# A token shift mixed ahead of the projections on GpSimd and VectorE, and the post units one step earlier

## The chip, the cores and the metric

One core of a Trainium2 chip runs the whole program. The metric is the device time of that core in microseconds (us), as a median of several executions. A second kind of record is one profiled execution, whose trace gives the start and length of every instruction. The engines are TensorE (PE in the rows, with its weight loads as PEld), VectorE (DVE), ScalarE (ACT), GpSimd (POOL) and SyncE (SP), which only issues transfers here. Each works through its own list in order and waits on semaphores.

## What is computed

Two blocks in a row, on x of 8 batches, 512 tokens, 128 channels, each followed by a residual sum and a layer norm. The first is a causal attention of 16 heads of 8 channels, whose score is a tanh of q times k plus two bias terms. The second is a feed-forward part with a token shift, and it is the one that changes:

```python
x_prev = jnp.concatenate([jnp.zeros((B, 1, C), x.dtype), x[:, :-1, :]], axis=1)
xr = mu_r * x + (1.0 - mu_r) * x_prev
xk = mu_k * x + (1.0 - mu_k) * x_prev
r = jax.nn.sigmoid(jnp.einsum('btc,dc->btd', xr, W_r))
k = jnp.einsum('btc,dc->btd', xk, W_k)
k_act = jnp.square(jax.nn.relu(k))
out = r * jnp.einsum('btc,dc->btd', k_act, W_v)
```

mu_r and mu_k are one number per channel.

## The kernel before, in words

The work of a batch is one *period* of 20 *steps* (PAIRS). Step t belongs to pair t of the batch: two score tiles of 128 keys by up to 512 queries, packed so that causal blocks that are empty are left out. A pair goes this way:

- *scores* on TensorE: q times k into one of three PSUM places (PSUM_PAIRS) of 1024 columns. It waits until *main* has read the pair that was in that place, three pairs before.
- *tanh* on ScalarE (L784), from PSUM to the tile probs.
- *biases* on TensorE, one step later (BIAS_LAG), into the same PSUM place. It waits for the tanh.
- *main* on VectorE (L1005): alpha times tanh plus biases.
- *exp* on ScalarE (L789), three steps after its tanh (EXP_LAG), so that tanh of pair t is followed by exp of pair t-3.
- *mask* on GpSimd (L893), in the same step as exp: zeros above the diagonal. It is one or two affine_select.
- *weighted sums* on TensorE (values_of), at the steps of VALUES_STEPS, into the tile sums.

On TensorE the scores of pair t+1 come last in step t, but at the steps of AHEAD_FIRST (2, 3, 4, 7, 9, 18) they come right behind the biases.

Beside the pairs, each period carries *side units*, all through one PSUM bank (side_bank), which the reader of a unit has to free before the next. The unit tables say at which step TensorE makes them:

- PREP_UNITS and VALUES_UNITS, for a later batch: xT2, q2, k2, F2 (features), G2 (lattice features), v1. What comes of q, k, J and G is cut into three bf16 parts: *hi* (VectorE, L1039), *rest* (GpSimd, L900: subtract), *mid* (VectorE, L1044), *lo* (GpSimd, L906: subtract). SyncE writes them to DRAM and loads them from there in another layout. The tables PREP in the GpSimd and VectorE programs give the steps.
- POST_UNITS, for the batch before: oT0 and oT1 (transposes of the sums, then *normalise*), aT (transpose of the attention output), y (output projection), x1T, kk, rr, kv. Their readers are in the tables POST: on VectorE *attn_out*, *residual* with *stats* and *moments*, *x1_out* (copy of x1T from PSUM, L1105), *gate* (L1111); on GpSimd *inv_std* (L914, L916: the reciprocal root), *norm* (L924, L928), *gated_residual* (L934).

So the path from y to the output of a batch runs y, residual, stats, moments, inv_std, norm, x1T, x1_out, kk and rr, relu and square and r_tanh on ScalarE, kv, gate, gated_residual, second stats, inv_std and norm.

The tile x1T has 1+512 columns, of which the first is zero, so x1T[:, 0:512] is the input shifted by one token. The setup scales each of the two weights twice, by mu and by 1-mu (w_r_mix, w_k_mix), and kk and rr are each a sum of two products, one with x1T and one with its shifted view. All are in fp32, and each product of 512 columns stands in the trace as two matmul records. kk gives 512 tokens in one go; rr is made in four blocks of 128 tokens.

Which periods have what: period 0 has preparation and no post units. Periods 1 to 5 have all (periods 1 to 4 run in a hardware loop of two periods a turn). Period 6 and 7 have post units and no preparation, period 7 no values either. The feed-forward part of the last batch stands behind the periods, in two halves of 256 tokens, with code and semaphores of its own (tail).

In the setup VectorE's instructions are linked: each waits for the one before (link). The copies and scalings of the weights stand in front of x_out(1), which feeds the second batch's q, k and features.

## Time and profile before

| what | us |
|---|---|
| median of 3 runs | 443.48 |
| lowest and highest | 440.82, 444.28 |
| the profiled execution, whole | 439.53 |
| its span, first to last instruction | 437.5 |

The page of the profile gives the busy time of each engine, with its share of the span and its instructions:

```profile
PE 368.5 (84%) x2907; PEld 190.6 (44%) x2907; DVE 328.5 (75%) x539; ACT 327.2 (75%) x364; POOL 230.4 (53%) x367
```

and the span in 40 slices, each digit the busy share in tenths (9 is 90% or more):

```profile
PE   3657778808989999999999998999898999899863
DVE  4874778806797979788887889788977876697643
ACT  1012489915899888989898988898889998999712
POOL 4315337611388636963597349644965264435541
PEclk9855899957999999999999999999999999899978
```

The first quarter is setup and period 0, with a gap at about 90 to 100 us in which TensorE waits for a transfer. From about 100 to 412 us run the seven periods with post units, then the tail. TensorE's granted clock is full through the periods.

### The profile page before, as it was taken

The page shows a single profiled execution, that of the slowest core. Times are in us where ns is not written, and L with a number is a line of the kernel's source. Part 1 is how long each engine was busy: PE and PEld are TensorE (multiplying, and loading weights), DVE is VectorE, ACT ScalarE, POOL GpSimd, SP SyncE. Part 2 cuts the span into 40 slices and gives each one's busy share as a digit, 9 for nine tenths or more (in the row PEclk, how much of TensorE's full clock was granted, in tenths as well). Part 3 has the DMA queues.
Part 4 walks back from the last instruction along what each step waited for, and adds up shares of the span by engine and source line. Part 5 has one row for each costly group of instructions (what it writes and reads, how often), then busy time and mean ns, then how long its engine had stood idle before and what let it go on. Part 6 is the DMA issues. An engine that isn't in the chain of part 4 may idle for free.

```text
span 437.5 us, 8760 instructions
## 1 busy us (share of the span) xinstructions
PE 368.5 (84%) x2907; PEld 190.6 (44%) x2907; DVE 328.5 (75%) x539; ACT 327.2 (75%) x364; POOL 230.4 (53%) x367
## 2 busy tenths in 40 slices
PE   3657778808989999999999998999898999899863
PEld 1232333304446444544445354645353546344543
DVE  4874778806797979788887889788977876697643
ACT  1012489915899888989898988898889998999712
POOL 4315337611388636963597349644965264435541
PEclk9855899957999999999999999999999999899978
DMA  3357878678766376758763876676755751100000
GB/s 97 112 167 152 200 192 137 123 171 183 123 146 198 101 149 125 150 147 181 141 159 111 172 143 136 169 167 142 146 149 139 151 111 40 49 25 1 2 25 24
DMA packets 40272, 55.31 MB, mean 126 GB/s; under 512 B 3427, under 2 KB 38243, under 8 KB 38655
## 3 DMA queue, kind: packets, MB, share of 16 engines
q1 hardware_dynamic: 36542, 53.06, 52.9%
q10 hardware_dynamic: 3696, 1.84, 2.4%
q8 instruction: 18, 0.29, 0.3%
q14 instruction: 16, 0.12, 0.1%
HBM read 38.69 MB, written 16.19 MB: 125 GB/s over the span
## 4 chain that ended last, share of the span: by engine, by line
PE 42%; DVE 18%; issue 9%; POOL 9%; DMA 9%; SPq 6%; ACT 5%; ACTq 0%; DVEq 0%; POOLq 0%
PE raw L512 16%; PE side_bank L512 14%; PE sums L512 9%; DVE probs L1005 7%; DMA i_stack<-hamming_i 5%; SPq L413 3%; DMA k_rows<-parts 3%; ACT probs L789 3%; ACT probs L784 2%; POOL probs L893 2%; PE side_bank L599 2%; POOL x L928 2%; POOL x L924 2%; POOL parts L906 2%; DVE bn L1090 1%
## 5 line engine op out<-in xcount | busy, mean ns | idle before, releaser
L1005 DVE SCALAR_TENSOR_TENSOR probs<-probs,scal,raw 128x1024 f32<-128x1024 f32 x160 | 202.2, 1272 | 46.2 <-PE raw L512 45.7
L784 ACT ACTIVATE probs<-raw 128x1024 f32<-128x1024 f32 x160 | 163.9, 1025 | 52.0 <-PE raw L512 51.3
L893 POOL TENSOR_SCALAR_AFFINE_SELECT probs<-probs 128x256 f32<-128x256 f32 (+1 forms) x224 | 98.8, 459 | 150.7 <-ACT probs L789 150.2
L789 ACT ACTIVATE probs<-probs 128x1024 f32<-128x1024 f32 x160 | 169.3, 1059 | 0.9 <-DVE probs L1005 0.9
L512 PE MATMUL raw<-q_stack,k_stack 72*128 72x384 bf16 (+3 forms) x512 | 99.0, 306 | 17.3 <-DVE probs L1005 13.7
L512 PE MATMUL raw<-i_stack,j_stack 111*128 111x384 bf16 (+3 forms) x512 | 98.0, 304 | 15.1 <-DMA i_stack<-hamming_i 12.5
L512 PE MATMUL sums<-probs,values 128*32 128x256 f32 (+2 forms) x1280 | 93.0, 390 | 4.2 <-POOL probs L893 4.1
L512 PEld LDWEIGHTS raw<-q_stack,k_stack 72*128 72x128 bf16 x512 | 38.5, 99 | 71.3 <-DVE probs L1005 46.4
L512 PEld LDWEIGHTS raw<-i_stack,j_stack 111*128 111x128 bf16 x512 | 42.3, 98 | 60.2 <-issue 31.9
L512 PEld LDWEIGHTS sums<-probs,values 128*32 128x32 f32 x1280 | 29.5, 108 | 50.4 <-issue 26.0
L900 POOL TENSOR_TENSOR whole<-whole,parts 128x512 f32<-128x512 f32 x22 | 26.1, 1188 | 22.8 <-DVE parts L1039 22.8
L906 POOL TENSOR_TENSOR parts<-whole,parts 128x512 bf16<-128x512 f32 x30 | 35.1, 1172 | 4.2 <-DVE parts L1044 4.2
L1068 DVE COPY sums_sb<-sums 128x512 f32<-128x512 f32 x15 | 10.4, 691 | 19.9 <-PE sums L512 19.9
L1044 DVE CAST parts<-whole 128x512 bf16<-128x512 f32 x32 | 16.7, 522 | 2.9 <-POOL whole L900 2.8
L916 POOL TENSOR_TENSOR rstd<-var_eps,minus_half 128x4 f32<-128x4 f32 x14 | 14.7, 1047 | 1.2
L512 PEld LDWEIGHTS side_bank<-w_r_mix,x1T 128*128 128x128 f32 x112 | 13.6, 191 | 1.0
L797 ACT ACTIVATE feats<-side_bank 128x512 f32<-128x512 f32 x8 | 4.9, 612 | 12.1 <-PE side_bank L512 12.1
L512 PE MATMUL side_bank<-w_r_mix,x1T 128*128 128x128 f32 x112 | 13.6, 275 | 0.0
L1039 DVE CAST parts<-whole 128x512 bf16<-128x512 f32 x24 | 12.2, 508 | 1.9 <-DMA q_rows<-parts 1.6
L512 PE MATMUL side_bank<-x1T,w_k_mix 128*128 128x512 f32 x28 | 13.2, 591 | 0.0
L836 ACT ACTIVATE probs<-shift_col 1x1536 bf16<-1x1536 bf16 x1 | 1.5, 1481 | 14.9 <-DVE w_r_mix L1245 14.9
L1090 DVE BATCH_NORM_STATS2 bn<-res 128x6 f32<-128x128 f32 x56 | 12.2, 279 | 0.2
(144 smaller groups left out, 345.7 us busy)
## 6 DMA issues: line engine op xcount, KB each, us to landing
q_stack<-q_rows SPq DMA_DIRECT2D x21, 384.0 KB
k_stack<-k_rows SPq DMA_DIRECT2D x21, 384.0 KB
i_stack<-lattice_i SPq DMA_DIRECT2D x21, 288.0 KB
i_stack<-hamming_i SPq DMA_DIRECT2D x21, 288.0 KB
q_rows<-parts SPq DMA_DIRECT2D x8, 384.0 KB, 17.2
k_rows<-parts SPq DMA_DIRECT2D x8, 384.0 KB, 8.9
j_rows<-parts SPq DMA_DIRECT2D x8, 384.0 KB, 8.5
lattice_i<-parts SPq DMA_DIRECT2D x8, 288.0 KB
```

The source lines that it names most:

```text
L413: sp.dma_start(i_stack[par][at:at + rows, first:first + n], lattice_i[par].rearrange("l (e h) i -> (l e) (h i)", h=H)[:, first:first + n]) ...
L512: return nc.tensor.matmul(o, lhsT, rhs, start=start, stop=stop, **kw)
L784: nc.scalar.activation(pair_probs(t), raw[:, t % PSUM_PAIRS, :].rearrange("p (u i) -> p u i", u=2), ACT.Tanh).then_inc(tanh_done, 1)
L789: nc.scalar.activation(pair_probs(t), pair_probs(t), ACT.Exp).then_inc(exp_done, 1)
L893: last = nc.gpsimd.affine_select(out=v, in_=v, compare_op=ALU.is_ge, fill=0.0, base=0, pattern=[[0, v.shape[1]], [1, P]], channel_multipli ...
L900: nc.gpsimd.tensor_tensor(whole[:, kind, :], feats[:] if kind == J else whole[:, kind, :], parts[:, kind, 0, :], ALU.subtract).then_inc(re ...
L906: nc.gpsimd.tensor_tensor(parts[:, kind, 2, :], whole[:, kind, :], parts[:, kind, 1, :], ALU.subtract).then_inc(lo_done[kind], 1)
L916: nc.gpsimd.tensor_tensor(rstd[:], var_eps[:], minus_half[:], ALU.pow).then_inc(rstd_done, 1)
L1005: v.scalar_tensor_tensor(out=o, in0=o, scalar=scal[:, 2:3], in1=raw[:, t % PSUM_PAIRS, :].rearrange("p (u i) -> p u i", u=2), op0=ALU.mult ...
L1039: v.tensor_copy(parts[:, kind, 0, :], feats[:] if kind == J else whole[:, kind, :]).then_inc(hi_done[kind], 1)
L1044: v.tensor_copy(parts[:, kind, 1, :], whole[:, kind, :]).then_inc(mid_done[kind], 1)
L1090: v.bn_stats(bn[:, blk, :], res[:, blk, :]).then_inc(bn_done, 1)
```

## The change

kk and rr become single products, of the unscaled weights (w_kT, w_rT) with inputs that are mixed beforehand: mix = x_prev + mu times (x - x_prev). The difference x - x_prev is one subtraction on GpSimd (*shifted*, tile shift_dif), the two mixes are scalar_tensor_tensor on VectorE (*mix*, for k first). They are written into tiles that are free at that time, attnT and the second half of sums_sb. kk and rr wait for the mixes (mix_done) where they waited for x1_out. The setup gets two more copies, of the unscaled weights; the scaled ones stay, for the tail, which is unchanged.

The post units from aT on move one step forward, v1 one back, G2 one forward. The tables of VectorE and GpSimd are set anew, for the preparation too. The core of the diff:

```diff
-PREP_UNITS = {0: ["xT2"], 2: ["q2"], 3: ["k2"], 5: ["F2"], 12: ["G2"]}
+PREP_UNITS = {0: ["xT2"], 2: ["q2"], 3: ["k2"], 5: ["F2"], 11: ["G2"]}
...
-VALUES_UNITS = {7: ["v1"]}
+VALUES_UNITS = {8: ["v1"]}
-POST_UNITS = {1: ["oT0"], 6: ["oT1"], 8: ["aT"], 10: ["y"], 14: ["x1T"], 16: ["kk"], 17: ["rr"], 18: ["kv"]}
+POST_UNITS = {1: ["oT0"], 6: ["oT1"], 7: ["aT"], 9: ["y"], 13: ["x1T"], 15: ["kk"], 16: ["rr"], 17: ["kv"]}
...
+        shift_dif = sb("shift_dif", [P, T])
+        mixed = [attnT[:], sums_sb[:, 1, :]]
...
-                    pe.wait_ge(dve_freed, side_units.through(b, "x1T"))
-                    mm(o, w_k_mix[0][:], x1T[:, 1:1 + T], stop=False)
-                    last = mm(o, w_k_mix[1][:], x1T[:, 0:T], start=False)
+                    pe.wait_ge(mix_done[1], pv + 1)
+                    last = mm(o, w_kT[:], mixed[1])
                 elif use == "rr":
-                    pe.wait_ge(dve_freed, side_units.through(b, "x1T"))
-                    for n in range(JB):
-                        mm(o[:, n * P:(n + 1) * P], x1T[:, 1 + n * P:1 + (n + 1) * P], w_r_mix[0][:], stop=False)
-                        last = mm(o[:, n * P:(n + 1) * P], x1T[:, n * P:(n + 1) * P], w_r_mix[1][:], start=False)
+                    pe.wait_ge(mix_done[0], pv + 1)
+                    last = four(o, mixed[0], w_rT[:])
...
+            def shifted(n):
+
+                pool.wait_ge(dve_freed, side_units.through(n + 1, "x1T"))
+                nc.gpsimd.tensor_tensor(shift_dif[:], x1T[:, 1:1 + T], x1T[:, 0:T],
+                                        ALU.subtract).then_inc(dif_done, 1)
...
-            PREP = {6: [(rest, Q)], 10: [(lo, Q), (rest, K)], 13: [(lo, K), (rest, J)], 14: [(rest, G)],
-                    16: [(lo, J)], 17: [(lo, G)]}
...
+            PREP = {6: [(rest, Q)], 8: [(lo, Q)], 11: [(rest, K)], 12: [(rest, J)], 14: [(rest, G)], 15: [(lo, K)],
+                    16: [(lo, J)], 18: [(lo, G)]}
...
+            def mix(n):
+
+                dve.wait_ge(dif_done, n + 1)
+                for which in (1, 0):
+                    v.scalar_tensor_tensor(out=mixed[which], in0=shift_dif[:], scalar=mu[:, which:which + 1],
+                                           in1=x1T[:, 0:T], op0=ALU.mult, op1=ALU.add).then_inc(mix_done[which], 1)
...
+            PREP = {0: [(x_out,)], 2: [(projected, Q)], 3: [(projected, K)], 5: [(hi, Q)], 7: [(mid, Q)], 10: [(hi, K)],
+                    11: [(features_i,), (hi, J)], 12: [(mid, K), (hi, G)], 15: [(mid, J)], 16: [(mid, G)]}
...
+                link(v.tensor_copy((w_rT, w_kT)[n][:], src))
```

How the lists stand on the engines, at three places of a full period. The first is GpSimd, behind the first half of the normalisation of x1: the rest of it, the masks, and the bf16 cutting of J, K and G. Before:

```order
L928 TENSOR_TENSOR x<-x,rstd 128x512 [waits centred,rstd_done]
L890 REGISTER_ALU
L893 AFFINE_SELECT probs<-probs 128x4x128 [waits exp_done]
L890 REGISTER_ALU
L893 AFFINE_SELECT probs<-probs 128x2x128 [waits exp_done]
L906 TENSOR_TENSOR parts<-whole,parts 128x512 [waits mid_done1]
L900 TENSOR_TENSOR whole<-feats,parts 128x512 [waits hi_done2]
```

and after:

```order
L930 TENSOR_TENSOR x<-x,rstd 128x512 [waits centred,rstd_done]
L892 REGISTER_ALU
L895 AFFINE_SELECT probs<-probs 128x2x128 [waits exp_done]
L895 AFFINE_SELECT probs<-probs 128x2x128
L902 TENSOR_TENSOR whole<-whole,parts 128x512 [waits hi_done1]
L892 REGISTER_ALU
L895 AFFINE_SELECT probs<-probs 128x4x128 [waits exp_done]
L902 TENSOR_TENSOR whole<-feats,parts 128x512 [waits hi_done2]
L892 REGISTER_ALU
L895 AFFINE_SELECT probs<-probs 128x2x128 [waits exp_done]
L935 ISA
L936 TENSOR_TENSOR shift_dif<-x1T 128x512 [waits dve_freed]
```

The normalisation is now followed by mask 8 (the two pieces), rest K (L902 with hi_done1), mask 9, rest J and mask 10, and then the new subtraction (L936). Before, rest K stood ahead of the root, and mask 8 between the root and the normalisation, where mask 7 stands now.

The second is VectorE from step 12 on, between the mains (probs). Before:

```order
L1005 SCALAR_TENSOR_TENSOR probs<-probs,scal,raw 128x1024 [waits tanh_done,bias_ready]
L1039 CAST parts<-whole 128x512 [waits scratch_in3,dve_freed]
L1002 REGISTER_ALU
L1005 SCALAR_TENSOR_TENSOR probs<-probs,scal,raw 128x1024 [waits tanh_done,bias_ready]
L1016 REGISTER_ALU
L1105 COPY x1T<-side_bank 128x512 [waits dve_unit]
L1068 COPY sums_sb<-sums 128x512 [waits pv_done]
L1002 REGISTER_ALU
L1005 SCALAR_TENSOR_TENSOR probs<-probs,scal,raw 128x1024 [waits tanh_done,bias_ready]
```

and after:

```order
L1053 CAST parts<-whole 128x512 [waits rest_done1]
L1048 CAST parts<-whole 128x512 [waits scratch_in3,dve_freed]
L1011 REGISTER_ALU
L1014 SCALAR_TENSOR_TENSOR probs<-probs,scal,raw 128x1024 [waits tanh_done,bias_ready]
L1025 REGISTER_ALU
L1114 COPY x1T<-side_bank 128x512 [waits dve_unit]
L1011 REGISTER_ALU
L1014 SCALAR_TENSOR_TENSOR probs<-probs,scal,raw 128x1024 [waits tanh_done,bias_ready]
L1120 SCALAR_TENSOR_TENSOR sums_sb<-shift_dif,mu,x1T 128x512 [waits dif_done]
L1120 SCALAR_TENSOR_TENSOR attnT<-shift_dif,mu,x1T 128x512
```

mid K (L1053, waits rest_done1) is new in this place, and the two mixes (L1120) stand behind the main of pair 13, in front of the copy of the sums and the main of pair 14. They wait for the subtraction.

The third is TensorE around kk. Before:

```order
L512 MATMUL raw<-q_stack,k_stack 128x512 [waits scores_done]
L512 MATMUL raw<-q_stack,k_stack 128x512
L550 REGISTER_ALU
L512 MATMUL raw<-i_stack,j_stack 128x512 [waits tanh_done]
L512 MATMUL raw<-i_stack,j_stack 128x512
L610 REGISTER_ALU
L512 MATMUL side_bank<-x1T,w_k_mix 128x512 [waits dve_freed]
L512 MATMUL side_bank<-x1T,w_k_mix 128x512
L568 REGISTER_ALU [waits mask_done]
L512 MATMUL sums<-probs,values 32x256 [waits sums_read]
L512 MATMUL sums<-probs,values 32x256 x3
```

and after:

```order
L517 MATMUL raw<-i_stack,j_stack 128x256 [waits tanh_done]
L517 MATMUL raw<-i_stack,j_stack 128x256 x3
L615 REGISTER_ALU
L517 MATMUL side_bank<-sums_sb,w_kT 128x512 [waits mix_k_done,dve_freed]
L517 MATMUL sums<-probs,values 32x256 [waits mask_done]
L517 MATMUL sums<-probs,values 32x256 x3
L517 MATMUL raw<-q_stack,k_stack 128x512 [waits scores_done]
L517 MATMUL raw<-q_stack,k_stack 128x512
L555 REGISTER_ALU
L517 MATMUL raw<-i_stack,j_stack 128x512 [waits tanh_done]
L517 MATMUL raw<-i_stack,j_stack 128x512
```

kk is one product, waits for the mix of k, and stands ahead of the scores of pair 16 (the 128x512 q_stack row behind it); before, those scores stood ahead of kk.

## Rows read from the trace of the kernel before

**Rows 1.** Table of stretches: stretch, length, busy us (count) per engine, PEclk, DMA.

```profile
241.00:286.00 45.00, 42.66 (x361) 22.42 (x360) 38.15 (x61) 39.84 (x44) 28.85 (x45) 1.00 0.69 151
```

**Rows 2.** Groups by line and form: engine, names, shapes, count, busy us, mean ns, idle.

```profile
L512 PE MATMUL side_bank<-w_r_mix,x1T 128*128 128x128 f32 x112 | 13.6, 275 | 0.0
...
L512 PE MATMUL side_bank<-x1T,w_k_mix 128*128 128x512 f32 x28 | 13.2, 591 | 0.0
...
L900 POOL TENSOR_TENSOR whole<-whole,parts 128x512 f32<-128x512 f32 x22 | 26.1, 1188 | 22.8 <-DVE parts L1039 22.8
...
L1111 DVE SCALAR_TENSOR_TENSOR gated<-r_tanh,side_bank 128x512 f32<-128x512 f32 x7 | 4.8, 687 | 0.7
```

**Rows 3.** Timeline, ScalarE: start, length, instruction, and in brackets the idle time before.

```profile
235.47 1.03 ACT L784 ACTIVATE probs<-raw 128x1024 f32<-128x1024 f32 x1 [1.06 <-PE raw L512]
...
255.40 1.02 ACT L784 ACTIVATE probs<-raw 128x1024 f32<-128x1024 f32 x1 [1.53 <-PE raw L512]
...
272.11 0.60 ACT L799 ACTIVATE k_act<-side_bank 128x512 f32<-128x512 f32 x1
...
273.28 1.01 ACT L784 ACTIVATE probs<-raw 128x1024 f32<-128x1024 f32 x1
...
275.92 1.02 ACT L784 ACTIVATE probs<-raw 128x1024 f32<-128x1024 f32 x1
...
277.77 1.03 ACT L784 ACTIVATE probs<-raw 128x1024 f32<-128x1024 f32 x1
...
280.72 1.02 ACT L784 ACTIVATE probs<-raw 128x1024 f32<-128x1024 f32 x1 [0.98 <-PE raw L512]
```

**Rows 4.** Timeline, TensorE: scores of pair 9, x1T, kk.

```profile
254.76 0.60 PE L512 MATMUL raw<-q_stack,k_stack 72*128 72x256 bf16 x4
...
266.84 0.63 PE L599 MATMUL side_bank<-ident,x 128*128 128x128 f32 x4 [0.46 <-POOL x L928]
...
270.17 1.88 PE L512 MATMUL side_bank<-x1T,w_k_mix 128*128 128x512 f32 x4
```

**Rows 5.** Timeline, VectorE: main of pair 9, residual, moments, mid K, x1_out.

```profile
258.39 1.26 DVE L1005 SCALAR_TENSOR_TENSOR probs<-probs,scal,raw 128x1024 f32<-128x1024 f32 x1
259.58 0.68 DVE L1102 TENSOR_TENSOR res<-side_bank,x_res 128x512 f32<-128x512 f32 x1
...
261.32 0.38 DVE L1097 BATCH_NORM_AGGREGATE mean_var<-bn 128x2 f32<-128x6 f32 x4 [0.15 <-DVE bn L1090]
...
262.79 0.42 DVE L1044 CAST parts<-whole 128x512 bf16<-128x512 f32 x1
...
268.08 0.68 DVE L1105 COPY x1T<-side_bank 128x512 f32<-128x512 f32 x1
```

**Rows 6.** Timeline, GpSimd: inv_std, norm of x1, masks 9 and 10.

```profile
262.37 0.25 POOL L914 TENSOR_SCALAR var_eps<-mean_var 128x4 f32<-128x4 f32 x1
...
264.45 1.05 POOL L924 TENSOR_TENSOR x<-res,mean_var 128x512 f32<-128x512 f32 x1
...
266.64 1.19 POOL L893 TENSOR_SCALAR_AFFINE_SELECT probs<-probs 128x512 f32<-128x512 f32 x2
```

**Rows 7.** Timelines of VectorE, TensorE and ScalarE in period 6.

```profile
347.74 0.68 DVE L1102 TENSOR_TENSOR res<-side_bank,x_res 128x512 f32<-128x512 f32 x1
...
357.85 1.88 PE L512 MATMUL side_bank<-x1T,w_k_mix 128*128 128x512 f32 x4
...
368.47 1.02 ACT L784 ACTIVATE probs<-raw 128x1024 f32<-128x1024 f32 x1 [1.06 <-PE raw L512]
```

**Rows 8.** The chain that ended last: start, length, what; then TensorE's timeline.

```profile
31.15 0.30 DVE w_vT L1247
...
78.27 21.64 DMA i_stack<-hamming_i
...
100.04 1.03 PE L512 MATMUL raw<-i_stack,j_stack 111*128 111x512 bf16 x2 [12.53 <-DMA i_stack<-hamming_i]
```

**Rows 9.** Timelines of GpSimd and VectorE in the setup: the subtraction beside a cast.

```profile
22.85 1.53 POOL L906 TENSOR_TENSOR parts<-whole,parts 128x512 bf16<-128x512 f32 x1 [2.79 <-DVE parts L1044]
...
23.40 1.26 DVE L1044 CAST parts<-whole 128x512 bf16<-128x512 f32 x1
```

16 lines of the change are left out of this document (9 added, 7 removed).

## The prediction

> **What bounds the kernel now.** I read the table of stretches first, then the timeline of each engine over one of the five full periods of the loop. In the 45 us from 241 to 286, TensorE is busy 42.66, ScalarE 39.84, VectorE 38.15, GpSimd 28.85 [rows 1]. A matmul's end is modelled, so 95% for TensorE doesn't say that its work is the limit. ScalarE has 39.84 of work and so about 5.2 us of waiting, and every one of its longer waits is for scores from TensorE. It gives the period its pace: tanh and exp of a pair take 1.85 us, start to start (275.92 to 277.77) [rows 3]. A period is 45.25 us, from tanh of pair 0 at 235.47 to the next at 280.72 [rows 3].
>
> Where do ScalarE's waits stand? 1.06 us before pair 0, 1.53 before pair 9 (255.40), 0.98 before the next pair 0 (280.72), the rest in small pieces [rows 3]. Around the two projections that the change halves, ScalarE hardly waits: from the relu at 272.11 on to the tanh at 277.77 it works through, and 0.98 is what it waits at the end [rows 3]. So two engines are full there at once, and what TensorE saves is worth only what ScalarE waits.
>
> The second thing to see is the chain that feeds the feed-forward part, on three in-order engines: y on TensorE, residual and statistics on VectorE (259.58 to 261.70), reciprocal root and normalisation on GpSimd (262.37 to 266.64), the transpose x1T on TensorE, which sat 0.46 us for it (266.84), then kk at 270.17 [rows 4, 5, 6]. This chain already ends a wait on TensorE.
>
> **The change, part by part.** I use three points of a period: R, where VectorE starts the residual (259.58), K, where kk starts (270.17), T, the next tanh of pair 0 (280.72). Before: R to K 10.6, K to T 10.55 [rows 3, 4, 5].
>
> TensorE loses half of kk and of rr: 13.2 and 13.6 us in 7 periods, so 1.89 and 1.94 each, and half of both is 1.9 us a period [rows 2]. GpSimd gains one 128x512 subtraction of two SBUF tiles: the like one (L900) takes 1.19 on average [rows 2]. VectorE gains two 128x512 scalar_tensor_tensor that read SBUF alone. No row shows this exact form in the loop; the nearest is the gate, 0.69 with one PSUM input [rows 2]. I take 0.69, 1.38 for both. ScalarE's work is unchanged.
>
> *R moves.* y goes to step 9, where its TensorE place is in front of what used to be step 10. The scores of pair 9, on which ScalarE waited the 1.53, keep their place: between them and step 6 stand the same products, only in another order (aT before, v1 after the two groups of weighted sums). They start at 254.76 [rows 4]. Scores 9 and biases 8 at no more than 0.6 each end at 255.96, main of pair 8 on VectorE takes 1.19 (258.39 to 259.58), so R comes at about 257.1, 2.5 earlier [rows 4, 5]. The casts moved on VectorE (mid and hi of Q and K) are in other gaps of it and cost nothing there.
>
> *R to K grows.* Statistics 2.12 (259.58 to 261.70) [rows 5]. GpSimd, now free, goes on at once: 2.08 for the root and the mask behind it (262.37 to 264.45; mask 8 there, mask 7 after, both of two pieces), 2.19 for the normalisation (to 266.64) [rows 6]. Up to here R+6.4. But what stood ahead of the normalisation on GpSimd now stands behind it: mask 8 (a mask of two pieces is about 0.7 of those 2.08), rest K 1.19, masks 9 and 10 1.19 (the two of 266.64), rest J 1.19, and only then the new subtraction, 1.19 [rows 2, 6]. By GpSimd alone: 6.4+0.7+4x1.19 = R+11.9, and with the first mix (0.69) kk starts at R+12.6. By VectorE it is a little later: its mid K, at step 12, waits for rest K at R+8.3, while VectorE would be there at R+6.9 (2.12, three mains at 1.19, and 1.2 for two casts and a copy between them). It stands 1.4 us with main of pair 12 queued behind. Then two casts 0.7 (0.42 each, their ends overlapped), main 12 1.19, the x1T copy 0.68, the subtraction 1.2, the mix 0.7 [rows 2, 5]: R+12.85. I take 12.85, so K is at 270.0 where it was at 270.17, though its place in the program is one pair earlier. That is the core of my forecast: the chain and not TensorE sets when kk starts, and the step forward is paid back as an idle TensorE ahead of kk, with the scores of pair 16 queued behind it and ScalarE waiting for those, and for kk's relu, about 1.2 us.
>
> *K to T.* kk alone 0.95, relu and square 1.17 (272.11 to 273.28), then ScalarE works through four pairs and r_tanh. From 273.28 to 277.77 it did two pairs and r_tanh with 0.19 of waiting, 4.49, so four pairs and r_tanh are 4.3+3.7 = 8.0 [rows 3]. Together 10.2 against 10.55: the halved rr and the 0.98 wait give 0.35, and no more. A further 0.1 to 0.2 may come at pair 1.
>
> A full period: -2.5+2.25-0.35 = -0.6 us, 44.65. Five of them: -3.0.
>
> *The last two periods* have no preparation, so no rest K and no rest J on GpSimd. R there is 347.74, kk 357.85, T 368.47 with 1.06 of waiting [rows 7]. R moves 1.7 earlier (pair 9 waited less there). R to K: R+6.4 for the normalisation, transpose and copy to R+7.7, masks to R+8.3, subtraction to R+9.5; but main of pair 13 holds VectorE until R+10.2 because its biases came late behind the waiting transpose, so kk at R+10.9, against 10.1. ScalarE is then still busy with the pairs before, and T comes 0.9 earlier, pair 1 about 1.7. I take 1.3: -2.6 for two.
>
> *Setup.* Two more 128x128 copies out of PSUM stand in the linked chain before x_out(1); the like one takes 0.30 and 0.02 to 0.04 between them. That chain runs on into the DMA that TensorE waits for until 100.04, 78.27 to 99.91 [rows 8]. So +0.7 at most, 0 if a full DMA queue swallows it. I take 0.7. The last batch's feed-forward part, behind the loop, is as before.
>
> Sum: -3.0-2.6+0.7 = -4.9 us on the profiled execution of 439.5, which gives 434.6. That execution is 4 us under the median of the runs shown, 443.48; on the median the same difference gives 438.6.
>
> **A rule against the change.** In the setup a GpSimd tensor_tensor took 1.53 (its like in the loop 1.19) and a cast on VectorE beside it took 1.26, where it takes 0.42 otherwise [rows 2, 5, 9]. So a VectorE operation can be held for up to 0.84 us beside GpSimd. Both mixes run while GpSimd goes on to mask 11 and rest G. If the first is held so, kk is 0.84 later. The Trainium skill, "GPSIMD Engine Reference", section "Key points", says that GpSimd shares its SBUF interfaces with VectorE and contends with instructions of two SBUF inputs, which the mixes are and the gate (0.69) is not; by it the mixes cost more than the row I used. The trace bears the contention out for casts; the one two-input form can't be separated there.
>
> **The rivals.**
> A, *TensorE was the limit.* For it: 42.66 of 45 busy. Against it: ScalarE doesn't wait around kk and rr. If GpSimd's chain is shorter than my sum, or VectorE has slack where I have none, the whole 1.9 us a period comes out, 7 times: -13.3+0.7, 430.9. Chance 0.2.
> B, *the mixes are held by GpSimd*: +0.84 on R to K in seven periods, +5.9 on my forecast, 444.5, no change. Chance 0.12.
> C, slower: *VectorE and GpSimd wait for each other.* In a full period K may be at most R+13.45 before the period gets longer than it was. If the subtraction slips behind one more exp (mask 10 ahead of it waits for exp 10, the mix holds the mains, they hold the exps), one pair's time, 1.85, is lost in each full period: -0.6+1.85 = +1.25, five times +6.2, and with nothing gained in the last two +6.9 in all: 450.4. Against it: exp 10 is over about 2 us before its mask's turn by my order of things. Chance 0.18.
> My forecast, 0.5.
>
> **How the numbers follow.** About 1% (4.4 us) is what a measurement can tell here. My -4.9 stands just beyond it, so the forecast's half divides 0.3 faster, 0.2 same. Faster: 0.3+0.2 = 0.5. Same: 0.2+0.12 = 0.32. Slower: 0.18. The forecast's own range is 435.5 to 442; with A at 430.9 and B at 444.5 inside and half of C cut off, 430 to 446.
>
> **What would show it.** In the changed profile: TensorE idle 1 to 1.7 us ahead of kk with the mix as releaser, ScalarE's wait moved from pair 0 to the relu or pair 16; VectorE idle about 1.4 us before mid K for rest K; R at pair 9's main, GpSimd without a gap from the root to the subtraction; kk one record pair instead of two, rr 8 records; the mixes 0.69. Period near 44.65, kk to kk. If TensorE doesn't wait for the mix and the period is near 43.4, A holds. If the mixes take over 0.9, B. If kk comes later than R+13.45, C. My forecast is wrong if R is not 2 us earlier relative to T.

## The result, and the profile after

The changed kernel takes 467.19 us (median of 4 runs, 463.74 to 471.20) where the kernel before takes 442.15 (4 runs, 435.68 to 444.28): a ratio of 1.063, with a 95% interval of 1.041 to 1.085. Some executions of a kernel fall in a slower state of the chip (the profiled ones of the changed kernel, of mixing alone, of mid K at 13 and of rr at 14 on VectorE did); every ratio here compares the other executions alone, and so isn't the quotient of the two medians beside it. Forecast were 438.6 us and a range of 430 to 446. The profiled execution took 471.2 us, its span 469.5 against 437.5, so the traces have 32.0 us to explain. This execution is the slowest of the four. The medians are 25 us apart and the ratio stands for 27.8 us, so 4 to 7 of the 32.0 are scatter between executions.

The page of the changed kernel: busy time by engine, and the row of TensorE's granted clock in 40 slices.

```profile
PE 375.0 (80%) x2837; PEld 185.9 (40%) x2837; DVE 348.5 (74%) x555; ACT 329.0 (70%) x364; POOL 241.5 (51%) x374
...
PEclk9856899858979999789979998899978999999997
```

TensorE has 70 records fewer and yet is busy 6.5 us longer (375.0 against 368.5). That can't be work; the last row says what it is: a 7 or 8 in nine of the slices 10 to 39, where the row of before has three. The table of stretches over one full period (columns as in [rows 1]: stretch, length, busy us and count of TensorE, its weight loads, VectorE, ScalarE and GpSimd, the clock, the DMA) puts it in its place:

```profile
254.70:277.00 22.30, 21.43 (x177) 11.26 (x175) 18.68 (x24) 19.97 (x22) 10.23 (x19) 1.00 0.65 142
...
286.30:291.20 4.90, 1.48 (x6) 0.64 (x6) 4.90 (x6) 3.11 (x4) 3.29 (x5) 0.77 0.61 114
291.20:296.00 4.80, 4.76 (x16) 1.60 (x17) 3.09 (x3) 1.93 (x3) 3.21 (x4) 0.52 0.57 125
296.00:304.00 8.00, 7.22 (x79) 4.34 (x77) 6.92 (x16) 7.45 (x9) 5.55 (x8) 1.00 0.33 118
```

From 286.3 to 291.2 TensorE works 1.48 us of 4.90, while VectorE is busy all the time. In the 4.8 us after it TensorE is busy throughout at a clock of 0.52, which is nearly all at the lower of its levels, 1.2 GHz. ScalarE has 3.11 and 1.93 us of work in these two stretches together of 9.7; in all of [rows 1] it waited some 5 us in 45. The timelines of the same period, engine by engine. ScalarE, to be held against [rows 3]:

```profile
254.75 1.03 ACT L786 ACTIVATE probs<-raw 128x1024 f32<-128x1024 f32 x1 [1.72 <-PE raw L517]
...
289.19 1.02 ACT L786 ACTIVATE probs<-raw 128x1024 f32<-128x1024 f32 x1 [1.75 <-PE raw L517]
...
293.32 0.60 ACT L801 ACTIVATE k_act<-side_bank 128x512 f32<-128x512 f32 x1 [2.17 <-PE side_bank L517]
...
295.30 1.02 ACT L786 ACTIVATE probs<-raw 128x1024 f32<-128x1024 f32 x1 [0.72 <-PE raw L517]
...
305.41 1.03 ACT L786 ACTIVATE probs<-raw 128x1024 f32<-128x1024 f32 x1 [1.65 <-PE raw L517]
```

TensorE, to be held against [rows 4]:

```profile
283.40 0.63 PE L604 MATMUL side_bank<-ident,x 128*128 128x128 f32 x4 [0.78 <-POOL x L930]
...
288.53 0.62 PE L517 MATMUL raw<-q_stack,k_stack 72*128 72x512 bf16 x2 [2.30 <-DVE probs L1014]
...
291.24 2.04 PE L517 MATMUL side_bank<-sums_sb,w_kT 128*128 128x512 f32 x2 [1.24 <-DVE sums_sb L1120]
...
304.77 0.61 PE L517 MATMUL raw<-q_stack,k_stack 72*128 72x512 bf16 x2 [1.55 <-DVE probs L1014]
```

VectorE, to be held against [rows 5] (residual, mid K, hi G, main of pair 12, x1T, the two mixes, second statistics, main of pair 18):

```profile
276.60 0.69 DVE L1111 TENSOR_TENSOR res<-side_bank,x_res 128x512 f32<-128x512 f32 x1 [0.16 <-PE side_bank L517]
...
285.15 0.83 DVE L1053 CAST parts<-whole 128x512 bf16<-128x512 f32 x1 [1.60 <-POOL whole L902]
285.91 1.37 DVE L1048 CAST parts<-whole 128x512 bf16<-128x512 f32 x1
287.20 1.27 DVE L1014 SCALAR_TENSOR_TENSOR probs<-probs,scal,raw 128x1024 f32<-128x1024 f32 x1
288.39 0.68 DVE L1114 COPY x1T<-side_bank 128x512 f32<-128x512 f32 x1
...
290.23 0.87 DVE L1120 SCALAR_TENSOR_TENSOR sums_sb<-shift_dif,mu,x1T 128x512 f32<-128x512 f32 x1
291.02 1.64 DVE L1120 SCALAR_TENSOR_TENSOR attnT<-shift_dif,mu,x1T 128x512 f32<-128x512 f32 x1
...
302.12 0.88 DVE L1099 BATCH_NORM_STATS2 bn<-res 128x6 f32<-128x128 f32 x4 [0.55 <-POOL res L942]
...
303.45 1.26 DVE L1014 SCALAR_TENSOR_TENSOR probs<-probs,scal,raw 128x1024 f32<-128x1024 f32 x1
```

GpSimd, to be held against [rows 6] (rest K, mask, rest J, then the new subtraction, mask, rest G):

```profile
283.96 1.16 POOL L902 TENSOR_TENSOR whole<-whole,parts 128x512 f32<-128x512 f32 x1
285.08 0.63 POOL L895 TENSOR_SCALAR_AFFINE_SELECT probs<-probs 128x512 f32<-128x512 f32 x1
285.68 1.32 POOL L902 TENSOR_TENSOR whole<-feats,parts 128x512 f32<-128x512 f32 x1
...
289.16 1.04 POOL L936 TENSOR_TENSOR shift_dif<-x1T 128x512 f32<-128x512 f32 x1 [1.61 <-DVE x1T L1114]
290.14 0.41 POOL L895 TENSOR_SCALAR_AFFINE_SELECT probs<-probs 128x256 f32<-128x256 f32 x1
290.52 1.59 POOL L902 TENSOR_TENSOR whole<-whole,parts 128x512 f32<-128x512 f32 x1
```

There are two stalls. **The first**: VectorE stands 1.60 us for rest K (until 285.15), and from the start of its first cast to the start of the main of pair 12 behind them pass another 2.05 us. TensorE has its scores of pair 15 waiting for that main, and stands 2.30 us. Then kk waits 1.24 more for the subtraction and the mix, and runs at half clock: two records take 2.04 us, about as long as the four of before at full clock (1.88, [rows 4]). What the change saved on kk is not there. **The second**: at 302.12 the second statistics stand on VectorE ahead of the main of pair 18. The next period's scores of pair 0 take the place in raw that this main frees; TensorE stands 1.55 us ahead of 304.77.

The last two periods, against [rows 7], in the timelines of VectorE, TensorE and ScalarE:

```profile
377.15 0.69 DVE L1111 TENSOR_TENSOR res<-side_bank,x_res 128x512 f32<-128x512 f32 x1
...
388.52 1.10 PE L517 MATMUL side_bank<-sums_sb,w_kT 128*128 128x512 f32 x2 [0.80 <-DVE sums_sb L1120]
...
400.59 1.02 ACT L786 ACTIVATE probs<-raw 128x1024 f32<-128x1024 f32 x1 [1.70 <-PE raw L517]
```

The first stall isn't there (no rest K, no rest J) and kk is really halved, 1.10 us. The second is there in full, 1.70 before pair 0. In the setup, against [rows 8], TensorE is released by the transfer at 99.42, where it was at 100.04:

```profile
99.42 1.03 PE L517 MATMUL raw<-i_stack,j_stack 111*128 111x512 bf16 x2 [11.58 <-DMA i_stack<-hamming_i]
```

With kk as a mark (starts in the timelines at 137.19, 188.15, 240.97, 291.24, 341.87, 388.52, 433.18; before at 133.65, 178.98, 224.84, 270.17, 315.59, 357.85, 400.61) the 32.0 us divide so: 3.5 up to the first kk, 22.7 over four full periods (51.17 against 45.49 each), 6.3 over the two that end with the last kk, and -0.6 behind it. The 3.5 are -0.6 up to the release above and +4.2 from there to the first kk, which aren't taken apart here. The release alone scatters from 92.7 to 102.2 over the traces of all the kernels below.

### The profile page after: what moved, and what is told of

Same layout as the page of the kernel before. It is cut to its first block, busy times and chain, and to the rows that moved or that the text cites. A ratio compares the mean times of both kernels' runs of the same rounds, so it can differ in the third digit from the quotient of the medians.

```text
span 469.5 us, 8647 instructions
## 1 busy us (share of the span) xinstructions
PE 375.0 (80%) x2837; PEld 185.9 (40%) x2837; DVE 348.5 (74%) x555; ACT 329.0 (70%) x364; POOL 241.5 (51%) x374
## 4 chain that ended last, share of the span: by engine, by line
PE 38%; DVE 22%; issue 10%; DMA 8%; POOL 8%; ACT 7%; SPq 5%; DVEq 0%; POOLq 0%; ACTq 0%
PE raw L517 15%; PE side_bank L517 12%; PE sums L517 9%; DVE probs L1014 8%; ACT probs L791 5%; DMA i_stack<-hamming_i 4%; SPq L418 3%; DMA k_rows<-parts 3%; DVE parts L1048 2%; POOL probs L895 2%; PE side_bank L604 2%; POOL res L942 2%; DVE bn L1099 2%; ACT probs L786 2%; POOL whole L902 1%
## 5 line engine op out<-in xcount | busy, mean ns | idle before, releaser
L895 POOL TENSOR_SCALAR_AFFINE_SELECT probs<-probs 128x256 f32<-128x256 f32 (+1 forms) x224 | 100.5, 462 | 160.4 <-ACT probs L791 160.3
L517 PE MATMUL raw<-q_stack,k_stack 72*128 72x384 bf16 (+3 forms) x512 | 103.0, 315 | 32.8 <-DVE probs L1014 30.6
L517 PE MATMUL raw<-i_stack,j_stack 111*128 111x384 bf16 (+3 forms) x512 | 102.2, 313 | 14.3 <-DMA i_stack<-hamming_i 11.6
L517 PE MATMUL sums<-probs,values 128*32 128x256 f32 (+2 forms) x1280 | 96.5, 402 | 1.5 <-POOL probs L895 1.3
L902 POOL TENSOR_TENSOR whole<-whole,parts 128x512 f32<-128x512 f32 x22 | 28.3, 1285 | 24.0 <-DVE parts L1048 24.0
L1053 DVE CAST parts<-whole 128x512 bf16<-128x512 f32 x32 | 18.3, 573 | 10.0 <-POOL whole L902 9.9
L517 PE MATMUL side_bank<-sums_sb,w_kT 128*128 128x512 f32 x14 | 12.4, 984 | 8.7 <-DVE sums_sb L1120 8.7
L1048 DVE CAST parts<-whole 128x512 bf16<-128x512 f32 x24 | 15.1, 628 | 0.9 <-DMA q_rows<-parts 0.7
L604 PE MATMUL side_bank<-ident,x 128*128 128x128 f32 x56 | 8.8, 279 | 6.9 <-POOL x L930 5.4
L517 PE MATMUL side_bank<-xT,wqT 128*128 128x512 f32 x14 | 10.6, 848 | 3.4 <-DVE xT L1029 2.9
```

Source lines behind the costliest of these rows:

```text
L517: return nc.tensor.matmul(o, lhsT, rhs, start=start, stop=stop, **kw)
L604: last = nc.tensor.transpose(o[:, n * P:(n + 1) * P], src(n), ident[:])
L895: last = nc.gpsimd.affine_select(out=v, in_=v, compare_op=ALU.is_ge, fill=0.0, base=0, pattern=[[0, v.shape[1]], [1, P]], channel_multipli ...
L902: nc.gpsimd.tensor_tensor(whole[:, kind, :], feats[:] if kind == J else whole[:, kind, :], parts[:, kind, 0, :], ALU.subtract).then_inc(re ...
L1048: v.tensor_copy(parts[:, kind, 0, :], feats[:] if kind == J else whole[:, kind, :]).then_inc(hi_done[kind], 1)
L1053: v.tensor_copy(parts[:, kind, 1, :], whole[:, kind, :]).then_inc(mid_done[kind], 1)
```

## The experiments

Fifteen kernels, in four groups; each group ran on one chip, beside the kernel before, and its ratios are against those runs. Beside each ratio with its 95% interval stand the starts of the first and the fifth kk in the trace, the mean period between them (their difference by 4), and the longest repeated waits of TensorE within a full period, in us. A wait named kk or rr stands ahead of that product; a number alone is a wait for a main where it is over 1, and for a mask or the normalised x1 where it is under. The four ratios of the first group (statistics at 19, mid K at 13, steps alone, mixing alone) rest on only three executions of the kernel before. The periods are those of one trace each.

| kernel | us | ratio [interval] | 1st, 5th kk | period | TensorE's wait |
|---|---|---|---|---|---|
| before | 437.07 to 442.15 | 1 | 133.65, 315.59 | 45.49 | 0.56 |
| after | 467.19 | 1.063 [1.041, 1.085] | 137.19, 341.87 | 51.17 | 2.30, 1.55, kk 0.8 to 1.7 |
| statistics at 19 | 453.90 | 1.043 [1.034, 1.053] | 129.99, 327.71 | 49.43 | 2.30, kk 0.8 to 1.7 |
| mid K at 13 | 456.53 | 1.044 [1.030, 1.058] | 135.00, 331.72 | 49.18 | kk 2.21, 1.54 |
| both moves | 443.47 | 1.018 [1.006, 1.030] | 131.33, 316.74 | 46.35 | kk 2.21 |
| both, rest G later | 442.05 | 1.013 [1.002, 1.023] | 131.43, 318.22 | 46.70 | kk 2.21 |
| steps alone | 464.69 | 1.070 [1.056, 1.084] | 132.00, 333.36 | 50.34 | 2.30, 1.54 |
| steps alone, repaired | 434.99 | 0.993 [0.990, 0.997] | 131.08, 310.47 | 44.85 | 0.79 |
| mixing alone | 460.62 | 1.047 [1.033, 1.062] | 139.91, 336.52 | 49.15 | kk 3.46 |
| zeros, too many | 459.30 | 1.051 [1.038, 1.064] | 135.05, 333.30 | 49.56 | 1.49 |
| zeros, sized | 454.69 | 1.037 [1.030, 1.045] | 133.16, 327.56 | 48.60 | 1.49, kk 0.81 |
| rr alone mixed | 434.60 | 0.993 [0.988, 0.998] | 127.74, 308.07 | 45.08 | 0.54, rr 0.25 |
| same, on VectorE | 433.37 | 0.991 [0.988, 0.995] | 134.94, 316.15 | 45.30 | 0.54 |
| repaired, rr at 15 | 457.29 | 1.047 [1.042, 1.052] | 128.29, 320.33 | 48.01 | rr 2.31 |
| repaired, rr at 14 | 438.51 | 0.998 [0.994, 1.002] | 131.71, 313.06 | 45.34 | 1.01 |
| same, on VectorE | 437.14 | 0.994 [0.990, 0.998] | 134.91, 316.25 | 45.34 | 1.01 |
| both mixed, on VectorE | 451.62 | 1.031 [1.027, 1.036] | 136.12, 329.00 | 48.22 | kk 3.05 |

### Which part of the change loses: steps alone, mixing alone

Steps alone: the tables of the changed kernel, the products of before, no subtraction and no mixes.

```diff
-                    pe.wait_ge(mix_done[1], pv + 1)
-                    last = mm(o, w_kT[:], mixed[1])
+                    pe.wait_ge(dve_freed, side_units.through(b, "x1T"))
+                    mm(o, w_k_mix[0][:], x1T[:, 1:1 + T], stop=False)
+                    last = mm(o, w_k_mix[1][:], x1T[:, 0:T], start=False)
...
```

> The changed kernel's tables with the products as before (two for kk, sixteen records for rr), no subtraction and no mixes. Theory P (the tables' places are most of the loss: statistics ahead of main 18, mid K waiting for rest K): the mixes' chain of about 2.7 us ahead of kk is gone, but 1.9 us of products are back and both waits stay; about 455 to 460. Theory M (the mixing is the loss): about 442, as before, or less.

464.69 us, ratio 1.070: theory P in kind, though it had expected 455 to 460. The loss is there whole with nothing of the mixing. VectorE's wait (1.60) and casts (0.83, 1.37) are the same, and so is TensorE's wait of 2.30 ahead of the scores of pair 15. In the timeline of TensorE and in the table of stretches of this kernel, one of the periods in which the four products of kk took twice their time:

```profile
281.19 1.04 PE L517 MATMUL raw<-q_stack,k_stack 72*128 72x512 bf16 x2 [2.29 <-DVE probs L1017]
...
282.87 3.62 PE L517 MATMUL side_bank<-x1T,w_k_mix 128*128 128x512 f32 x4
```

```profile
281.00:287.00 6.00, 5.81 (x18) 2.16 (x18) 1.92 (x3) 2.44 (x3) 2.69 (x4) 0.50 0.52 103
```

In two of the five full periods kk takes 3.62, in the others 1.88, and the wait ahead of the scores of pair 15 is 2.29 to 2.30 in all five.

Mixing alone: the tables of before, the products of the changed kernel; the subtraction is last at step 14 of GpSimd, behind rest G, the mixes at step 15 of VectorE.

```diff
-            POST = {10: [(inv_std, 0)], 11: [(norm, 0)], 18: [(gated_residual,)], 19: [(inv_std, 1), (norm, 1)]}
+            POST = {10: [(inv_std, 0)], 11: [(norm, 0)], 14: [(shifted,)], 18: [(gated_residual,)],
+                    19: [(inv_std, 1), (norm, 1)]}
...
```

> The new projections (subtraction on GpSimd at step 14, mixes on VectorE at 15, single products) in the tables of before. Theory P: kk is held by mask 11, rest G, subtraction and mix, about 1 to 2 us a period late, rr and kk are 1.9 us shorter; 442 to 450. Theory M (the mixing is the loss): 460 or more. Theory A (TensorE was the limit and only the tables spoil it): 430 to 435.

460.62 us, ratio 1.047: by its number this is theory M, by its place theory P, for it is kk that is held, and longer than the 1 to 2 us expected. So either part loses by itself, and the two don't add: TensorE stands 3.46 us ahead of kk in each full period, VectorE 0.93 for the subtraction.

### Undoing one place at a time

The second statistics back behind the main of pair 18 (step 19 of VectorE), the rest as changed:

```diff
-                    17: [(gate,)], 18: [(stats, 1, 0), (stats, 1, 1), (moments, 1)]}
+                    17: [(gate,)], 19: [(stats, 1, 0), (stats, 1, 1), (moments, 1)]}
```

> The changed kernel, with VectorE's second statistics back at step 19, behind main of pair 18. Theory P (a place in VectorE's list): the scores of the next period's pair 0 wait for main of pair 18, which the changed kernel puts behind the statistics; TensorE stood 1.54 us there. With the statistics behind it again this wait goes, about 1.5 us a period in seven periods: 10 us less than the changed kernel's 467, about 457. Theory Q (the late kk is the whole loss, what comes behind it is late in any case): within 3 us of 467.

453.90 us, ratio 1.043. The wait ahead of pair 0 is gone in every full period, the first stall stays (2.30, kk 2.05): theory P, with 13 us by the medians and 9 by the ratios for its 10. The period falls by 1.74.

Mid K one step later on VectorE, behind the main of pair 12, hi G where it is:

```diff
-                    11: [(features_i,), (hi, J)], 12: [(mid, K), (hi, G)], 15: [(mid, J)], 16: [(mid, G)]}
+                    11: [(features_i,), (hi, J)], 12: [(hi, G)], 13: [(mid, K)], 15: [(mid, J)], 16: [(mid, G)]}
```

> The changed kernel, with mid K on VectorE one step later (13), so that hi G and main of pair 12 no longer wait for rest K. Theory P: VectorE's 1.60 us wait in each of the five full periods goes, kk comes 1 to 1.5 us earlier, TensorE's 2.3 us gap ahead of the scores of pair 15 shrinks below 1 and the granted clock stays full around kk, which gives about another 1 us: 2 to 2.5 us a period, 455 to 458. Theory G (GpSimd's list, not the wait of VectorE, sets when kk starts): 464 or more.

456.53 us, ratio 1.044. The 2.30 ahead of the scores of pair 15 is gone, but the time appears ahead of kk, 2.21 us, and kk still takes 2.05 in three of five periods (1.29 and 1.34 in the others). Theory P had the time right and two of its steps wrong: it expected an earlier kk and a full clock around it. The period falls by 1.99.

Both, the two diffs above together:

> The changed kernel with both repairs: second statistics at step 19 and mid K at step 13. Theory P (the two places cost independently): 13 us from the one and 11 from the other off 467, so about 443, level with the kernel before. Theory S (the two share one loss, since each kernel's period is ended by the same chain): 450 or more.

443.47 us, ratio 1.018, as theory P had it. The period falls by 4.82, more than 1.74 and 1.99 together. (The ratios fall by 2.0, 1.9 and 4.6 points, and their intervals of one to two points each don't part 4.6 from the sum; the 1.1 us a period more is read from one trace of each.) Part of the reason is in the stretches behind the wait ahead of kk, which is 2.21 to 2.22 us in both kernels. First mid K alone moved (wait up to 282.0), then both (wait up to 271.3):

```profile
279.80:282.00 2.20, 0.02 (x1) 0.00 (x0) 1.57 (x3) 2.11 (x3) 2.20 (x4) 0.83 0.58 100
282.00:287.00 5.00, 4.97 (x16) 1.77 (x17) 3.29 (x4) 2.14 (x3) 3.20 (x4) 0.50 0.65 108
```

```profile
269.00:271.30 2.30, 0.09 (x2) 0.04 (x1) 1.67 (x3) 2.18 (x3) 2.30 (x4) 1.00 0.86 200
271.30:277.00 5.70, 5.70 (x44) 3.27 (x45) 5.38 (x7) 4.54 (x7) 4.45 (x7) 1.00 0.69 150
```

After the same wait the clock is 0.50 in the one and 1.00 in the other; kk takes 2.05 against 1.10 (1.10 to 1.49 in the five periods), and ScalarE waits 2.21 and 0.71 ahead of the relu and of pair 16 against 1.25 and nothing. These two periods are the extremes. In the 5 us from the start of kk on, the clock is 0.50, 0.66, 0.67, 0.50 and 0.66 in the five full periods with mid K alone moved, and 1.00, 0.66, 0.66, 1.00 and 0.66 with both.

The kernel with both moves prices the clock by itself. Its kk starts at 131.33, 176.79, 224.31, 271.30 and 316.74. The two periods that begin with kk at full clock last 45.46 and 45.44 us, the two that begin with 0.66 last 47.52 and 46.99, all behind the same wait of 2.21. So the fallen clock costs 1.5 to 2.1 us each time here, and where it stays up the period is no longer than before (45.49), in spite of the wait. The next kernel below agrees: one period of 45.44 that begins at full clock, and 46.85 to 47.53 for the three that begin at 0.66 to 0.69.

Rest G of GpSimd one step later than in that, behind the mixes:

```diff
-            PREP = {6: [(rest, Q)], 8: [(lo, Q)], 11: [(rest, K)], 12: [(rest, J)], 14: [(rest, G)], 15: [(lo, K)],
+            PREP = {6: [(rest, Q)], 8: [(lo, Q)], 11: [(rest, K)], 12: [(rest, J)], 15: [(rest, G), (lo, K)],
```

> Both repairs, and GpSimd's rest G moved from step 14 to 15, so that no two-input GpSimd operation stands beside the mixes. Theory Po (the second mix is held by rest G): the mix of r falls from 1.64 to 0.87 us or less, 0 to 0.8 us a period less than with both repairs alone. Theory W (a mix is 1.64 by itself): it stays.

442.05 us, ratio 1.013. The second mix falls from 1.64 to 0.74 us, so GpSimd's rest G had held it. The first stays at 0.87 and kk waits 2.21 as before; the intervals don't part the two kernels, and in the traces the period is 0.35 longer, with the clock at 1.00 behind kk in one period of five where it was in two. What holds the second mix costs nothing that can be measured, since rr comes a pair later.

### What the clock costs: products that add zero

To part the wait from the clock that falls with it, TensorE was given something to do in the wait: products with a matrix of zeros, added to the weighted sums. They don't shorten any wait. First four ahead of the scores of pair 15 and two ahead of kk, in the five full periods:

```diff
+            def fill(times):
+                for _ in range(times):
+                    nc.tensor.matmul(sums[:], zero_w[:], xT[0][:], start=False, stop=False,
+                                     skip_group_check=True)
...
+                        if t == 14 and post and prep:
+                            fill(4)
...
+                    if t == 15 and post and prep:
+                        fill(2)
```

> The changed kernel, with TensorE's waits ahead of the scores of pair 15 (2.30 us) and ahead of kk (0.8 to 1.7 us) filled by products that add zero to the sums (four and two of 512 columns, 0.95 us each pair at most), in the five full periods. The work that matters is the same. Theory Cl (the granted clock falls after the 2.3 us wait and costs kk 1.1 us and the products behind it another 1 us a period): the clock stays at 1.00 through kk, kk takes 0.95 to 1.1 instead of 2.04, and the whole comes 5 to 10 us under 467. Theory N (the lower clock stands beside the waits and costs nothing, since others are waited for): 467 or some us more, for the added products.

459.30 us, ratio 1.051, theory Cl. The fills were longer than the waits (3.70 and 1.88 us against 2.30 and 1.24) and put ScalarE 2.89 us behind ahead of pair 15, and still the period is 1.6 us shorter than the changed kernel's: kk takes 1.02. Then with fills that fit, two and one:

```diff
-                            fill(4)
+                            fill(2)
...
-                        fill(2)
+                        fill(1)
```

> The changed kernel with zero-adding products only as long as the waits that they stand in: two ahead of the scores of pair 15 (two take 1.85 us at the 3.70 us of the four in the earlier run, and the wait is 2.30) and one ahead of kk (0.94, and the wait is 1.24), in the five full periods; they add zero to the sums. Theory, the clock that falls after TensorE's wait costs a part of the loss: the granted clock stays at full speed through kk, kk's two records of about 1.0 us together instead of 2.04, the scores' wait of ScalarE ahead of pair 15 stays at 1.75 (it was 2.89 with four products), and the kernel is 8 to 12 us under the changed one, 455 to 459. Rival, only kk itself is longer at the low clock and what follows has slack: 1 us a period, 462 or more. Second rival, two products are too few and the clock falls all the same: no change from the changed kernel.

454.69 us, ratio 1.037. The same stretch, in the table and the timeline of TensorE:

```profile
275.00:286.00 11.00, 9.81 (x65) 5.10 (x64) 10.68 (x13) 8.00 (x11) 7.82 (x11) 1.00 0.52 135
```

```profile
273.99 1.98 PE L666 MATMUL sums<-xT,zero_w 128*128 128x512 f32 x4
276.36 0.61 PE L518 MATMUL raw<-q_stack,k_stack 72*128 72x512 bf16 x2 [0.39 <-DVE probs L1026]
```

The scores of pair 15 still wait for VectorE, but the clock stays full. The period is 48.60, 2.57 less than 51.17. Five full periods make 12.9 us, of the 32.0 that the traces differ by (the changed kernel's is of its slowest execution, 5.2 us above the mean of the others, so by an estimate of 5.2 over seven periods 2.57 may be 0.7 too high): about two fifths of the loss is the clock, not the waits themselves. The ratios give the same share, 2.6 of 6.3 points, but with an uncertainty of more than 2 points. The theory that priced the clock beyond kk holds, 12.5 us by the medians where it expected 8 to 12: kk alone accounts for 1 us of the 2.57.

### Is anything left for the change

Steps alone with both repairs (statistics at 19, mid K at 13, as in the diffs above):

> The moved tables with both repairs (VectorE's second statistics at step 19, its cast mid K at 13) and the products as before the change, no subtraction and no mixes. In the changed kernel the same two repairs took the time from 1.0634 to 1.0179 of before, with a wait of 2.21 us ahead of kk for the subtraction and the mix. Theory, the mixing costs what is left in that kernel, and a move by one step is worth little by itself: no wait ahead of kk over 0.5 us, kk's four records 1.9 us at full clock, and 0.985 to 1.00 of before. Rival, the moved tables have a further loss of their own: 1.005 or more, with a wait of TensorE over 1 us that no run has shown so far.

434.99 us, ratio 0.993, period 44.85: 0.64 less than before. The step forward of the post units does gain, if little (0.3 to 1.0% by the interval), once the two moved instructions no longer hold a main. Against it, both moves with the mixing has a period of 46.35, so that mixing both costs 1.5 us a period in these tables: 0.6 in the periods in which its clock stays up (45.45), the rest in the others. Its waits show for what:

```profile
PE side_bank L517 <- DVE sums_sb L1120: 12.6, 7, 2.2
```

(TensorE's waits: what waits, for what, us in total, times, longest.) kk waits 12.6 us in 7 periods for its mix.

rr alone mixed, kk from two products of x1T, in the tables of before: the subtraction at step 14 of GpSimd, one mix at step 16 of VectorE, rr at 17.

```diff
...
-                for which in (1, 0):
+                for which in (0,):
...
```

> The tables of before, kk as two products straight from x1T, and only rr as a single product of a mixed input (subtraction on GpSimd at 14, one mix on VectorE at 16). The chain ahead of kk is as before and 0.97 us of rr go. Theory P (what matters is what kk waits for): no gap ahead of kk, full clock, 436 to 443. Theory M (any mixing costs): 447 or more.

434.60 us, ratio 0.993, theory P, with a wait of 0.25 ahead of rr and none ahead of kk. The same with the subtraction on VectorE and the mix at step 15 (GpSimd's *shifted* and its place in the table are gone):

```diff
             def mix(n):
-                dve.wait_ge(dif_done, n + 1)
+                dve.wait_ge(dve_freed, side_units.through(n + 1, "x1T"))
+                v.tensor_tensor(shift_dif[:], x1T[:, 1:1 + T], x1T[:, 0:T],
+                                ALU.subtract).then_inc(dif_done, 1)
+                dve.wait_ge(dif_done, n + 1)
...
```

> The tables of before, kk from two products of x1T, rr alone mixed, and the subtraction on VectorE too, just ahead of its mix at step 15: GpSimd has no part in it. It tells apart what the hand-over to GpSimd costs from what VectorE's time costs. Theory, VectorE has room there and the hand-over is the cost: the same as the version with the subtraction on GpSimd (0.9931) or up to 0.5% under it. Rival, VectorE's own time sets the step: the subtraction takes 0.7 to 0.9 us more of it in each of seven periods, the main of the next pair comes that much later, and the ratio is 1.000 to 1.008.

433.37 us, ratio 0.991: the fastest here, though its interval overlaps those of rr with GpSimd and of the repaired steps. VectorE had the room.

Now rr alone mixed in the repaired tables, with the mix at step 15 and rr at 16 (the kernel with both moves, and of it):

```diff
-                    pe.wait_ge(mix_done[1], pv + 1)
-                    last = mm(o, w_kT[:], mixed[1])
+                    pe.wait_ge(dve_freed, side_units.through(b, "x1T"))
+                    mm(o, w_k_mix[0][:], x1T[:, 1:1 + T], stop=False)
+                    last = mm(o, w_k_mix[1][:], x1T[:, 0:T], start=False)
...
-                for which in (1, 0):
+                for which in (0,):
...
-                    9: [(residual,), (stats, 0, 0), (stats, 0, 1), (moments, 0)], 13: [(x1_out,)], 14: [(mix,)],
+                    9: [(residual,), (stats, 0, 0), (stats, 0, 1), (moments, 0)], 13: [(x1_out,)], 15: [(mix,)],
```

> The moved and repaired tables, kk from two products of x1T, and only rr mixed: the subtraction on GpSimd at step 13 and one mix on VectorE at step 15. With the tables of before the same half of the mixing gave 0.9931 of before. Theory, the two edits add up: kk waits for nothing, the mix takes 0.74 to 0.87, rr 1.13 instead of about 2.1, and 0.98 to 0.995. Rival, mid J and the mix stand together at step 15 on VectorE and the main of pair 15 and the tanh of rr come later: 1.00 or more.

457.29 us, ratio 1.047, as bad as mixing alone; the rival had named the step, and the theory was wrong. The waits and the timeline of TensorE:

```profile
PE side_bank L517 <- DVE attnT L1121: 15.2, 7, 2.3
```

```profile
278.28 2.05 PE L517 MATMUL side_bank<-w_rT,attnT 128*128 128x128 f32 x8 [2.31 <-DVE attnT L1121]
```

At step 15 the mix stands behind sums_out, which itself waits 1.79 us for TensorE's weighted sums, and behind a main and mid J; rr waits 2.31 us in the five full periods and 1.78 in the two others, and in the stretch behind the wait (278.3 to 282.0) the clock is 0.58. The same kernel with the mix at step 14, ahead of sums_out:

```diff
-                    9: [(residual,), (stats, 0, 0), (stats, 0, 1), (moments, 0)], 13: [(x1_out,)], 15: [(mix,)],
+                    9: [(residual,), (stats, 0, 0), (stats, 0, 1), (moments, 0)], 13: [(x1_out,)], 14: [(mix,)],
```

> As the version that took 1.0471 (moved and repaired tables, rr alone mixed, subtraction on GpSimd at 13), with its mix at step 14 of VectorE instead of 15, ahead of the sums of the half (a wait of 1.8 us) and the main of that step. Theory, only TensorE's wait of 2.3 us ahead of rr in seven periods and the low clock after it made that loss: rr waits for nothing, its eight products take 1.05 to 1.15 instead of 2.05, ScalarE's wait of 2.56 ahead of the tanh is gone, and the ratio is 0.985 to 0.998. Rival, mixing rr in the moved tables costs by itself: 1.02 or more.

438.51 us, ratio 0.998: 4.9 points for one step of one instruction. rr waits for nothing and takes 1.05; what is left is a wait of 1.01 us in each full period for a main, a few products later, that the kernel without the mix doesn't have. With the subtraction on VectorE too, by the same edit of *mix* as above:

> As the run before, with the subtraction on VectorE just ahead of the mix at 14, so that GpSimd has no part and VectorE waits for nothing. Theory: 0.983 to 0.996, the same as with GpSimd or up to 0.4% under it, since VectorE's wait for the subtraction (about 0.6) and its stretch of casts go. Rival, VectorE's time delays the next main: 1.00 or more.

437.14 us, ratio 0.994. The two gains (repaired steps 0.993, rr mixed 0.993 in the tables of before) don't add: neither combination tried came below either.

At last the whole mixing, with the subtraction on VectorE, in the repaired tables (the kernel with both moves, and the same edit of *mix*):

> The moved and repaired tables with the whole mixing, but the subtraction on VectorE, just ahead of the two mixes at step 14, instead of on GpSimd at 13. With the subtraction on GpSimd this version took 1.0179 of before, TensorE waited 2.2 us ahead of kk in five periods, VectorE itself only 0.6 for the subtraction. Theory, two mixes and a subtraction stand between the residual's x1T and kk whoever does them, and TensorE's wait of over 2 us with its lowered clock is the cost: VectorE gives 0.7 to 0.9 for the subtraction in place of the 0.6 wait, the wait ahead of kk stays at 1.8 to 2.4, and the ratio is 1.01 to 1.02. Rival, the hand-over to GpSimd and the casts that it stretches are the cost: the wait ahead of kk is under 1 us, the clock stays up, and the ratio is 0.99 to 1.00.

451.62 us, ratio 1.031, worse than the 1.018 with GpSimd. The hand-over to GpSimd isn't what costs; the first theory holds in kind and is too small in size (it had a wait of at most 2.4 ahead of kk and 1.02). VectorE and TensorE:

```profile
276.83 0.68 DVE L1108 COPY x1T<-side_bank 128x512 f32<-128x512 f32 x1
277.43 1.27 DVE L1008 SCALAR_TENSOR_TENSOR probs<-probs,scal,raw 128x1024 f32<-128x1024 f32 x1
278.62 0.86 DVE L1113 TENSOR_TENSOR shift_dif<-x1T 128x512 f32<-128x512 f32 x1
279.51 1.53 DVE L1117 SCALAR_TENSOR_TENSOR sums_sb<-shift_dif,mu,x1T 128x512 f32<-128x512 f32 x1
...
281.19 1.68 PE L517 MATMUL side_bank<-sums_sb,w_kT 128*128 128x512 f32 x2 [3.05 <-DVE sums_sb L1117]
```

GpSimd's subtraction had run beside the main of pair 13; on VectorE it stands behind it, and the first mix is held by rest G besides. kk starts 4.36 us after the start of the x1T copy, with GpSimd in the same tables 3.51 (267.79 to 271.30), and in the changed kernel 2.85 (288.39 to 291.24). Two products of x1T need only the copy. I take that to be why rr, which comes a pair later, bears the mixing and kk doesn't; no run moved kk itself to a later step.

## Why the prediction was wrong

I forecast a full period of 44.65 = 21.6 (T to R) + 12.85 (R to K) + 10.2 (K to T). From T 254.75, R 276.60, K 291.24, T 305.41 it is 50.66 = 21.85 + 14.64 + 14.17. The sum was -3.0 for five periods; measured, kk to kk, are 5.68 more in each.

**R moves: right.** 21.85 against 21.6.

**VectorE waits for rest K: right** in place and nearly in size, 1.60 against 1.4. But "with main of pair 12 queued behind" is where I stopped. I didn't ask who waits for that main. The scores of pair 15 do; I named only those of pair 16, behind kk. TensorE stood 2.30 us ahead of them.

**R to K: a term mis-sized.** The main of pair 12 starts 10.60 after R (287.20), and I had it at R+9.0: 8.3 for rest K, 0.7 for two casts. (These terms and those behind them add up to 12.77, not 12.85.) The wait for rest K ended at 8.55, and from the first cast's start to the main's it was 2.05. Behind the main there was little error: 1.19, then 2.85 for copy, subtraction and mix with what lies between them, where I had 2.6. The first mix was 0.87, not 0.69; so rival B's mechanism exists, but at the mixes it is worth 0.2, while the 1.35 us of it fell on two casts that I had priced at their undisturbed length, although I had quoted a cast of 1.26 beside GpSimd [rows 9] as the rule against the change. I applied it to the new instructions alone, and not to the moved ones.

**K to T: the step that failed**, 14.17 against 10.2. From kk to the relu 2.08 instead of 1.0, because kk ran at 1.2 GHz. From the relu to pair 16 1.98 instead of 1.17, with 0.72 of waiting for scores that TensorE made at that clock. From there through four pairs and r_tanh 8.46 instead of 8.0, with 0.31 of waiting for scores. And 1.65 ahead of pair 0, where I had set the wait to zero. These are 1.08+0.81+0.46+1.65 = 4.00, against parts that add up to 10.17. The 1.65 is a wait that I missed: the second statistics moved from step 19 to 18, from behind the main of pair 18 to ahead of it, and it waits for the gated residual besides (0.55). Moving them alone back takes 1.74 us off the period. The clock I never had as a term: I wrote that TensorE would stand ahead of kk for 1.2 us, and took it for the price. With the clock held up by the sized fills the full period was 2.57 shorter.

**The last two periods**: forecast -1.3 each. Last kk to kk is 44.66 against 42.76, +1.9. T to R fell by 0.8 where I had 1.7; R to K is 11.37 (forecast 10.9), fair; K to T is 12.07 against 10.62 before, with 1.70 of waiting ahead of pair 0 where there was 1.06, and I had expected no growth. The kk to kk ahead of it, 46.65 against 42.26, holds the K to T of the fifth full period (14.50 against 10.62) and so belongs to the stalls above.

**Setup**: forecast +0.7, or nothing if a queue swallows it. TensorE was released 0.6 earlier. With a release that scatters by some 10 us between the traces, this shows neither the 0.7 nor its being swallowed.

**The rivals.** A (TensorE was the limit, 430.9) isn't borne out: rr alone mixed halves rr, takes 0.8 us off TensorE (1.13 against 1.94) in each of seven periods, 5.7 in all, and the whole kernel gains 3.0 us (0.8 to 5.2 by the interval). B (the mixes held by GpSimd) is the 0.2 above, since the second mix, held longest, isn't waited for. C had the right sign and nearly the right neighbourhood, kk later than R+13.45 lengthens the period, and kk came at R+14.64. Its mechanism (the subtraction behind one more exp) isn't what happened: GpSimd stood idle for the x1T copy, 1.61 us, ahead of the subtraction.

On the held casts and mixes the Trainium skill, "GPSIMD Engine Reference", section "Key points", which I had cited, gives contention for VectorE instructions with two SBUF inputs and for those in a 2-port mode. The trace agrees for the first, 1.64 for a mix that takes 0.74 undisturbed, and casts are held too, 1.37 for one of 0.42; that a cast runs in a 2-port mode no row here shows. The Trainium skill, "SBUF — State Buffer", section "Who interferes with whom", says of VectorE's 2-port modes that whichever instruction is issued first has the shared ports for the whole of it, and the other fully blocks. By the rows that is so, for the casts and for the mixes, see the last section.

## What to carry to other kernels

When an instruction moves by one step in an in-order engine, write down what stood behind it there before and stands ahead of it now, and follow each of those to the engine that waits for it; both stalls here were a main that had come to stand behind a small instruction with a wait of its own. A wait of TensorE like those of 2.2 to 3.5 us here is to be priced with the clock it may lose, not by its length. Work taken off TensorE pays only where its replacement isn't on the chain that TensorE waits for: mixing ahead of the second consumer (rr) gained 0.7 to 0.9% in the tables of before, nothing beyond the repaired steps in theirs, and lost 4.7% one step too late; ahead of the first (kk) it lost in every place tried. All the gains here are under 1%.

## What the runs showed of the hardware

**VectorE held by GpSimd, to the end of the instruction.** The starts and lengths above fit one rule: a cast or mix that meets a running GpSimd instruction ends a fixed time after that one's end. Casts: 285.98 for a mask that ends at 285.71, and 287.28 for rest J's end at 287.00, +0.27 and +0.28. Mixes: 291.10 for the mask's end at 290.55, 292.66 for rest G's at 292.11, +0.55 both. In the kernel with both mixed on VectorE the mix that ends at 281.04 stands against a rest G of 278.90 to 280.49, +0.55 again. Over the traces of all the kernels here, all 444 casts that start beside a single GpSimd instruction of 128x256 or 128x512 end 0.26 to 0.37 us behind its end, and all 98 mixes 0.53 to 0.56. The exception is the root (128x4): a cast at 279.82 keeps its 0.42 inside the root's 279.23 to 280.28.

GpSimd is held the same way by a VectorE instruction that came first: rest J (from 285.68) ends 1.02 behind the end of the first cast (285.98), rest G (from 290.52) 1.01 behind that of the first mix (291.10), and they last 1.32 and 1.59 where rest K took 1.16.

The price is therefore what the instruction that came first has left, up to 1 us here, not a fixed factor. The one-input cast from f32 to bf16 is held as the two-input mix is; the mains and copies in these rows that read PSUM weren't (1.27 and 0.68 us beside GpSimd).

**The clock after a stop.** The same wait of 2.2 us ahead of the same product left the granted clock at 0.50, at 0.66 and at 1.00 over the 5 us behind it, in periods of two kernels that differ in one place of VectorE's table; the one with both moves alone has 1.00 twice and 0.66 three times. In steps alone it fell at kk in two of five like periods. It also fell behind shorter waits: behind two of the five of 1.5 to 1.6 us ahead of pair 0 in the changed kernel (at about 203.5 and 357.4), and once in the kernel before, at 376 in period 7, behind waits of 0.5 to 0.7 us. The length of the wait alone doesn't decide it. What does stays open. When it fell, it stayed down for 3 to 7 us.
